# One step's outputs behind one step's scores: the order of TensorE's work in the attention stage of a transformer block

## The reference, cut to what matters

```python
xm = layernorm(x) * (1 + sc_a) + sh_a            # sc_a, sh_a, ... from the condition
q, k, v = split(xm @ Wqkv)                       # (b, h, t, 32)
scores = einsum('bhqd,bhkd->bhqk', q, k) * 32 ** -0.5
scores = where(causal, scores, -inf)
out = einsum('bhqk,bhkd->bhqd', softmax(scores), v)
x = x + gt_a * (out @ Wproj + bproj)
x = x + gt_m * (gelu(xm2 @ W1 + b1) @ W2 + b2)   # xm2: layernorm and modulation again
```

## Time and profile before

| | |
|---|---|
| median of 3 runs | 2193.76 us |
| the profiled execution | 2191.45 us, span 2189.4 us |
| TensorE matmuls busy | 2137.5 us (98%) |
| VectorE | 1284.6 us (59%) |
| ScalarE | 928.9 us (42%) |
| POOL | 954.3 us (44%) |
| TensorE's share of the chain that ended last | 87% |

### The profile page before, as it was taken

The page is one execution under the profiler, slowest core; times in us unless marked ns, Lnnn a source line. Parts: engine busy times, 40 slices in busy tenths (PEclk is TensorE's granted clock), DMA queues, the critical chain, the costliest instruction groups (busy, mean ns, idle before and its releaser), DMA issues.

```text
span 2189.4 us, 30720 instructions
## 1 busy us (share of the span) xinstructions
PE 2137.5 (98%) x11326; PEld 1440.9 (66%) x11326; DVE 1284.6 (59%) x2872; ACT 928.9 (42%) x1780; POOL 954.3 (44%) x380
## 2 busy tenths in 40 slices
PE   6999999999999999999999999899999999999999
PEld 5888885454545545444545544687888888888887
DVE  4777876777777777777777756685312222122122
ACT  2111115565566656656566566435322222222222
POOL 2001007979889797997979784660000000000000
PEclk9999999999999999999999999999999999999999
DMA  6538347135252433635244224684201011011010
GB/s 231 211 138 295 130 154 193 36 93 122 65 131 55 109 73 70 142 69 118 56 96 98 69 69 127 204 316 153 76 31 58 1 58 58 1 58 47 11 39 20
DMA packets 129309, 223.28 MB, mean 102 GB/s; under 512 B 8574, under 2 KB 26054, under 8 KB 128968
## 3 DMA queue, kind: packets, MB, share of 16 engines
q1 hardware_dynamic: 108568, 180.43, 30.2%
q10 hardware_dynamic: 20592, 40.90, 5.0%
HBM read 146.31 MB, written 74.98 MB: 101 GB/s over the span
## 4 chain that ended last, share of the span: by engine, by line
PE 87%; DVE 5%; issue 2%; POOL 2%; DMA 2%; ACT 1%; SPq 0%; DVEq 0%; ACTq 0%; POOLq 0%; PEldq 0%
PE p_acc L1975 15%; PE m_hid L1961 15%; PE st L1445 12%; PE acc L860 12%; PE mx L1425 11%; PE o_ps L1462 11%; PE r_ps L1469 3%; PE p_acc L1940 3%; DVE part L1305 2%; POOL psum_k L1202 2%; DVE unused L1301 2%; PE r_ps L1483 1%; PE acc L836 1%; PE tp L824 1%; PE misc L814 1%
## 5 line engine op out<-in xcount | busy, mean ns | idle before, releaser
L1244 ACT ACTIVATE prob<-st 128x512 f32<-128x512 f32 (+3 forms) x1280 | 607.7, 544 | 385.5 <-PE st L1445 366.7
L1202 POOL TENSOR_TENSOR psum_k<-psum_k,prob 128x2048 f32<-128x2048 f32 (+1 forms) x150 | 662.8, 4419 | 20.0 <-ACT prob L1244 4.9
L1305 DVE TENSOR_REDUCE part<-mx 128x1 f32<-128x512 f32 x707 | 455.1, 684 | 83.3 <-PE mx L1425 81.8
L1445 PE MATMUL st<-q_st,k_st 98*128 98x512 f32 (+3 forms) x1280 | 484.0, 391 | 3.2 <-PE r_ps L1469 1.4
L1425 PE MATMUL mx<-k_st,qx_st 96*128 96x512 f32 (+3 forms) x1196 | 466.5, 406 | 13.9 <-DVE part L1305 3.5
L1862 DVE TENSOR_TENSOR m_g_lo<-m_g,m_g_hi 128x512 fp32r<-128x512 f32 x128 | 88.6, 692 | 477.2 <-ACT m_g_hi L1779 477.0
L1445 PEld LDWEIGHTS st<-q_st,k_st 98*128 98x128 f32 x1280 | 241.8, 189 | 184.9 <-issue 102.3
L1425 PEld LDWEIGHTS mx<-k_st,qx_st 96*128 96x128 f32 x1196 | 224.0, 189 | 168.2 <-DVE part L1305 101.4
L1301 DVE CUSTOM_DVE_ANT_0 unused<-mx,mask_row 128x512 bf16<-128x512 f32 (+2 forms) x489 | 228.1, 486 | 128.8 <-PE mx L1425 125.0
L1772 ACT ACTIVATE m_g<-m_hid,vcol 128x512 f32<-128x512 f32 x128 | 88.2, 689 | 469.1 <-PE m_hid L1961 469.1
L1462 PE MATMUL o_ps<-prob,v_sb 128*32 128x512 f32 (+3 forms) x2560 | 277.8, 539 | 0.8 <-POOL prob L1185 0.8
(11 more groups left out here) (186 smaller groups left out, 2576.0 us busy)
## 6 DMA issues: line engine op xcount, KB each, us to landing
k_st<-qk_scratch SPq DMA_DIRECT2D x96, 256.0 KB, 7.9
qx_st<-qk_scratch SPq DMA_DIRECT2D x96, 256.0 KB, 5.0
q_st<-qk_scratch SPq DMA_DIRECT2D x96, 256.0 KB
qk_scratch<-st_hi ACTq DMA_DIRECT2D x16, 1024.0 KB, 4.2
qk_scratch<-st_lo ACTq DMA_DIRECT2D x16, 1024.0 KB, 7.0
xs<-in_x_dram SPq DMA_DIRECT2D x8, 1024.0 KB, 9.1
v_sb<-v_scratch SPq DMA_DIRECT2D x8, 1024.0 KB, 16.1
o_scratch<-o_sb SPq DMA_DIRECT2D x32, 256.0 KB, 2.3
```

What stands on the lines that cost most here:

```text
L1202: nc.gpsimd.tensor_tensor(dst, src, prob[:, s % BUF, :, m:], ALU.add).then_inc(pool_added, 1)
L1244: nc.scalar.activation(prob[:, s % BUF, h, m:], st[n % RING][:, m:], ACT.Exp, scale=SCALE).then_inc(exp_done, 1)
L1305: nc.vector.tensor_reduce(most, bank[:, 0:w], AX.X, ALU.max).then_inc(mx_free, 1)
L1445: nc.tensor.matmul(st[n % RING][:, m:], k_st[u][0:MROWS, h, kt * P:(kt + 1) * P], q_st[0:MROWS, pos % 2, h, m:], start=True, stop=True).th ...
```

## The change

In `body` of TensorE, the outputs move into the loop over the two steps of a block:

```diff
@@ -1519,8 +1519,7 @@
                             if not after:
                                 pe.wait_ge(ones_ready, 1)
                             scores(g + 1, 1 - u, s - L.NS, between)
-                    for s in (2 * b - 2, 2 * b - 1):
-                        product(g, u, s, more)
+                        product(g, u, s - 2, more)
```

## The result

The changed kernel takes 2199.26 us (median of six runs, 2197.66 to 2201.79) beside 2191.03 us of the kernel before in the same series (2186.96 to 2194.2): +8.2 us, a ratio of 1.0037 with a 95% interval of 1.0024 to 1.0050. It is slower, by nearly twice the 4.4 us that the prediction took for the least that can be told from none. A second series, with eight runs beside 31, gives 1.0032 (1.0021 to 1.0043).

A forecast was written before the change was run, and what follows sets the result against it. POOL bounds the first two stretches of a group, TensorE waiting on its VectorE and ScalarE rings the third. The order's +3.0 and the clock's +5.2 us gave +8.2 on 2193.76, so 2202.0 us; range 2189 to 2214.

The forecast's parts named there:

- The three bounds of a group: Groups 2 to 6: three stretches, 53.79, 38.68 and 37.23 us, together changing by +0.1 us a group.
- a gain of 0.8: First stretch, first add to step 17's add: 53.0 us against 53.79, with TensorE waiting 1.3 us for step 12's mask.
- 38.68 stays: Second stretch, step 17's add to step 27's outputs: set by POOL, unchanged at 38.68 us.
- a loss of 0.9: Third stretch: blocks 15 to 19 win 0.25, but step 38's outputs push into block 20, 5.97 us for 4.82.
- the growth to 130 us or more: Sign of being right: distances between groups' first adds grow from 129.7 to 130 to 131.5 us.
- Half bursts and change-overs: TensorE's blocks: 0.33 us per added change-over, half bursts 2.54, single outputs 0.99; TensorE could win about 2.5 us a group.
- Group 0: First group: POOL stays full in its first stretch, so it has the third stretch's loss alone, +1.0 us.
- The last group: Halves win 0.07 a block, the wait for step 12's mask is 2.4, late blocks win nothing back: +2.0 us.
- ScalarE "at nothing": Half bursts: ScalarE has no backlog, so no cost; uncovered it would cost its present waits, 60.6 us in all.
- A fall in four of the six blocks 7 that had none: Block 7, groups 1 to 7: a wait over a microsecond lowers the clock, 4 x 1.3 = +5.2 us.
- The clock holds: +3.0: Rival: no added clock falls, only the order's +3.0 us, 2197 us, about no change; chance 0.25.
- the rival of 51 us: Rival: change-overs don't come back at all, 0.33 x 155 = 51 us, 2245 us; chance 0.05.

The follow-up runs named there:

- filled wait: Changed kernel plus eight extra matmuls ahead of step 12's outputs in the first and last group: 1.0016, +3.5 us over the kernel before.
- the kernel with the middle groups alone: New order in groups 1 to 6 only, old order in the first and last group: 0.9995 of the kernel before, -1.1 us.
- the repeated series: The changed kernel measured again without an edit, against 31 runs of the kernel before: 1.0032, +7 us.
- the first and last group alone: Two kernels, new order only in the first group or only in the last, against the kernel before: 1.0006 (+1.3 us) and 1.0015 (+3.3 us).
- the winning blocks: New order only in blocks 3-6, 11, 12, 15, 17 of groups 0 to 6: 0.9990 of the kernel before; with second matmuls in steps 14 and 15, 0.9972.
- the control: Kernel before plus a second full-width score matmul ahead of each narrow one of steps 14 and 15, groups 0 to 6: 1.0014, +3 us.

## Why the prediction was right, and where it wasn't

The time was right: +8.2 us forecast, +8.2 measured. That the number meets so closely is luck: several terms under it were off, and their errors cancel.

- **The three bounds of a group.** Right in size: "a gain of 0.8" in the first stretch came out as 1.0 (53.79 to 52.79), "38.68 stays" as 38.75, "a loss of 0.9" in the third as 0.8. Group 4 changed by -0.13 us where +0.1 was forecast, so the growth to 130 us or more that was named as a sign did not come. Two parts of it were off. TensorE wins less in blocks 1 to 6 than was worked out and comes later to step 12: it is idle for 0.39 us there, and not for the forecast 1.3. And the loss of 0.9 is itself two errors that cancel: block 20 takes 6.31 us from its first score to the add where 5.97 was worked out, and the blocks ahead of it win 0.7 and not 0.25.
- **Half bursts and change-overs.** Right for the block that was worked out in full (2.55 and 1.00 for 2.54 and 0.99). The list for the others was rougher: blocks 3 and 4 won 0.3 and 0.2 where 0.8 was forecast, block 12 nothing, while 13, 14 and 18 won 0.2 to 0.3 in group 4 where losses were forecast, and block 2 lost 0.4. It didn't matter where POOL is the bound.
- **Group 0.** Right without its fall: +0.9 for +1.0.
- **The last group.** Too small: +2.0 forecast, +3.9 without a fall (filled wait). The step that failed is ScalarE "at nothing". It holds where items stand between the scores, but the last group's late blocks have none, and they lose 2.0 us to the ring of scores (third stretch 40.53 to 42.58). What step 12's mask costs was put at 2.4 and is 2.2 (45.65 to 47.83); the halves won nothing before it and 0.3 in the second stretch. The price named for ScalarE, "60.6 us in all", measures nothing either: the waits put down to ScalarE grew by 126 us, and the time lost to them was about 2.
- **The clock.** "A fall in four of the six blocks 7 that had none" failed in place. In both traces of the changed kernel none of groups 1 to 6 falls. The wait of over a microsecond that was to bring these falls isn't there (0.39 us), so whether 1.3 us would do no run shows. Instead the falls in block 7 of the first and last group are the long ones (10.2 us in place of 3.4, and 3.4 or 6.8 where there was none), behind 2.9 and 1.6 us idle. By the first trace they cost 3.0 and 2.8 us, and group 1 lost a fall worth 1.6 (55.34 for 53.76 in the first stretch): 4.2 us where 5.2 was forecast. That both falls present before cost 1.27 us each was wrong for group 0, where POOL is the bound: its first stretch is 52.59 us with the fall, and 52.59 in the kernel with the middle groups alone, which has none there.
- **The rivals.** "The clock holds: +3.0" is what the filled kernel shows, +3.5. The change-overs cost nothing in the middle groups, so the rival of 51 us is out. The Trainium skill, "TensorEngine Tiling (Array Packing)", Key Properties, says that changing the tiling mode drains TensorE. The trace agrees that a change costs time: one step's outputs take 0.99 to 1.00 us, two in a row 1.86. It decides nothing by itself here.

Of the whole, 4.2 us are thus the order itself (0.9 + 3.9, less 0.6 in the middle groups; forecast 3.0) and the rest is clock, by the traces; by the medians the filled kernel splits the +7 of the repeated series as 3.5 and 3.5. Why the first and last group alone give 4.6 by their medians with the middle's -1.1, and not 7, is open but for the last group's shorter wait.

## What to carry to other kernels

Moving work between two bursts doesn't only cost its own length: ask what is due right behind it (here a chain of adds that starts a group's critical stretch) and which of its own inputs is then late. Alternating more finely halves the queue at the end of a burst but pays the start of every ring twice, so here it won where narrow pieces fall together and lost where a burst has little else in it. Apply such an order block by block, by what each block's timeline gives, and look at the granted clock of every block before believing a total: here falls had taken 4 of the 6 us that the winning blocks gave. And don't add up parts that were measured alone: one part can take away the wait on which another's loss rests.

## What was not expected of the hardware

More matmuls made a kernel faster: eight of them in a wait of up to 2.9 us kept TensorE's clock at 2.4 GHz and won some 3.5 us (+3.5 for +7). And a fall can repeat with the loop: with the new order in the winning blocks it came in block 7 of six groups in a row, at 522.9, 652.6, 782.3, 912.1, 1041.8 and 1171.5 us, 129.7 apart, which is the group's own length, while in the kernel before, whose block 7 has the same order, it came in two of eight. A fall that comes in every group looks like part of the group's own length. In the control the falls left block 7 and two turned up elsewhere, so keeping one block busy is no cure.
